# An eight-sequence language-model layer on one core: the first and the last steps reordered, and identity products in TensorE's gaps of the fill

## The reference

```
e0 = E0[tokens]; e1 = E1[tokens]                      # two embedding tables, 75 wide
p0 = e0 @ W0 + b0;  p1 = e1 @ W1 + b1                 # 64 wide
h  = softmax-weighted sum of p0 and p1 (logits p @ Wa + ba)
x  = layernorm(h)
q, k = x @ Q[h], x @ K[h]                             # 8 heads, 32 wide
h += sum over heads of softmax(q k^T / 8) @ x @ VO[h]
x2 = layernorm(h)
H  = gelu(x2 @ W1 + b1)                               # 256 wide
g  = softmax(H @ Wg + bg);  e = argmax(g)             # 8 experts
h += g[e] * (H @ Wd[e] + bd[e])
```

## Time and profile before

| | |
|---|---|
| median of 3 runs | 506.91 us (504.96, 506.91, 508.52) |
| the profiled execution: its own time | 509.85 us |
| its span, first to last instruction | 508.0 us |
| TensorE matmul busy | 461.6 us (91%) |
| VectorE busy | 339.7 us (67%) |
| ScalarE busy | 234.4 us (46%) |
| GpSimd busy | 204.3 us (40%) |
| DMA, mean rate | 61 GB/s |

### The profile page before, as it was taken

How to read it: one execution, slowest core, us unless ns; L and a number is a source line. 1 busy time by engine, 2 the same in 40 slices (tenths; PEclk the granted TensorE clock), 3 DMA queues, 4 the chain that set the end, 5 groups by cost and what they waited for, 6 DMA issues and landing times.

```text
span 508.0 us, 7112 instructions
## 1 busy us (share of the span) xinstructions
PE 461.6 (91%) x1920; PEld 248.5 (49%) x1920; DVE 339.7 (67%) x899; ACT 234.4 (46%) x448; POOL 204.3 (40%) x293
## 2 busy tenths in 40 slices
PE   2258999999899999999999999999999999989674
PEld 2236455455454655455545555555544554435251
DVE  4626857977776777768776778677677766722525
ACT  1012455565634474545644573448354653484020
POOL 8322211531427614462526432762046315521635
PEclk9999999999989999999999999999899999997957
DMA  6053313432232223122322223222212321000000
GB/s 144 0 134 90 76 37 85 115 74 64 64 87 50 65 67 101 34 59 68 84 52 65 63 75 87 65 63 68 69 30 66 81 73 40 10 12 0 1 10 10
DMA packets 24851, 30.94 MB, mean 61 GB/s; under 512 B 9196, under 2 KB 11500, under 8 KB 24812
## 3 DMA queue, kind: packets, MB, share of 16 engines
q1 hardware_dynamic: 22700, 27.25, 21.2%
q0 software_dynamic: 1536, 2.46, 2.1%
q10 hardware_dynamic: 576, 0.79, 0.6%
HBM read 3.99 MB, written 1.05 MB: 10 GB/s over the span
## 4 chain that ended last, share of the span: by engine, by line
PE 81%; DVE 6%; ACT 5%; issue 4%; ACTq 2%; POOL 1%; DMA 1%; SPq 1%; DVEq 0%; POOLq 0%
PE ctx_ps L780 24%; PE s_ps L760 13%; PE st_ps L769 12%; PE sh_ps L850 11%; PE sh_ps L827 6%; PE sh_ps L842 3%; PE sh_ps L804 3%; PE sh_ps L808 3%; PE sh_ps L787 2%; ACT L487 2%; PE sh_ps L809 2%; ACTq L201 1%; PE sh_ps L796 1%; DVE neg_max L512 1%; ACT prob L383 1%
## 5 line engine op out<-in xcount | busy, mean ns | idle before, releaser
L383 ACT ACTIVATE prob<-st_ps 128x512 f32<-128x512 f32 x256 | 138.9, 595 | 139.1 <-PE st_ps L769 137.5
L512 DVE TENSOR_REDUCE neg_max<-s_ps 128x1 f32<-128x512 f32 x256 | 164.7, 683 | 30.6 <-PE s_ps L760 29.4
L780 PE MATMUL ctx_ps<-prob,xa 128*64 128x512 f32 x512 | 140.9, 630 | 0.0
L760 PE MATMUL s_ps<-kst,qst 96*128 96x512 f32 x256 | 113.2, 488 | 6.7 <-DMA kst<-raw_k 4.2
L769 PE MATMUL st_ps<-qst,kst 98*128 98x512 f32 x256 | 86.8, 417 | 3.8 <-ACT prob L383 3.8
L760 PEld LDWEIGHTS s_ps<-kst,qst 96*128 96x128 f32 x256 | 47.9, 202 | 76.0 <-issue 33.1
L308 POOL TENSOR_TENSOR zsum<-z 128x256 f32<-128x256 f32 x31 | 23.0, 742 | 126.7 <-DVE z L595 126.7
L850 PE MATMUL sh_ps<-wd,hid 128*128 128x512 f32 x128 | 63.6, 627 | 0.3 <-DVE z L595 0.3
L769 PEld LDWEIGHTS st_ps<-qst,kst 98*128 98x128 f32 x256 | 50.0, 197 | 26.1 <-ACT prob L383 12.8
L639 DVE TENSOR_TENSOR yb<-sh_ps,bg_bd_s 128x512 f32<-128x512 f32 x32 | 22.1, 690 | 35.9 <-PE sh_ps L850 27.0
L780 PEld LDWEIGHTS ctx_ps<-prob,xa 128*64 128x64 f32 x512 | 25.7, 136 | 40.1 <-issue 32.9
(11 more groups left out here) (90 smaller groups left out, 484.2 us busy)
## 6 DMA issues: line engine op xcount, KB each, us to landing
qst<-raw_q SPq DMA_DIRECT2D x192, 64.0 KB, 2.0
kst<-raw_k SPq DMA_DIRECT2D x180, 64.0 KB, 2.0
qst<-shift_t SPq DMA_DIRECT2D x64, 4.0 KB
out<-res SPq DMA_DIRECT2D x8, 128.0 KB, 1.8
kst<-raw_k ACTq DMA_DIRECT2D x12, 64.0 KB, 2.2
rows<-emb,idx POOLq DMA_INDIRECT x32, 2.9
wd<-WdT SPq DMA_DIRECT2D x1, 512.0 KB, 5.1
w_raw<-weights SPq DMA_DIRECT2D x2, 192.0 KB, 3.8
```

Of the source, the lines that this page charges most:

```text
L383: AC.activation(prob[:, t % P_BUFS, :], st_ps[t % ST_BANKS][:, :], ACT.Exp, scale=-1.0).then_inc(p_done, 1)
L512: V.tensor_reduce(neg_max[:, n:n + 1], s_ps[(NT * b + n) % S_BANKS][:, :], AX.X, ALU.min).then_inc(max_done, 1)
L760: PE.matmul(s_ps[k % S_BANKS][:, :], qst[b % 2][0:3 * R, h, c * P:(c + 1) * P], kst[b % 2][0:3 * R, h, :], start=True, stop=True).then_inc ...
L780: last = PE.matmul(ctx_ps[d * C:(d + 1) * C, :], xa[b % 2][:, c, :], prob[:, (2 * m + d) % P_BUFS, :], start=(c == 0), stop=(c == J - 1))
```

## The change

At the start: the row of -1 in `kst` is written by GpSimd after `xa` of the first sequence and not after the first gather; VectorE builds `vox` (now `head_values`) after its copy of `e1_t` and not before the loop; `q1` and `k1` of sequence 0 are made at step -8 and not at -4, and VectorE takes both their parts; ScalarE's queue issues the keys of head 4 as well; the query stacks of heads 4 and 5 come earlier on SyncE's queue and apart from the key stacks, and sequence 0's `shift` goes ahead of the stacks of its step. The embedding of sequence 1 is done one to two steps later (`e0_t`, `e1_t` at step -2 and not -3; `p0`, `p1` at 0 and not -2), with its `blend` on VectorE and its `normal0` at the head of VectorE's step 2.

At the end: the expert products of sequence 6 are moved to steps 65 and 66, behind the last `vo`, and those of sequence 6 and 7 go into the banks `s_ps` and `st_ps` (`SPARE`), which are free once all maxima and exponentials are done; their evictions are items of their own (`ev0` to `ev3`), for sequence 6 at step 67, behind `normal1` of sequence 7; sequence 7's second layernorm, hidden layer, gate and routing are one step earlier; `yb` has four slots; VectorE takes two of the four mixes of sequence 6 too.

TensorE gets `keep_warm`: fp32 products of the 128x128 identity with itself into `ctx_ps`, which nothing reads before the first context. There are 12 before its loop, 3 after each of the first three quarters of the first `e0_t`, 20 after the first `p1` and 8 after the first `k1`: 49 in all.

```diff
@@ -48,13 +48,25 @@
-OTHERS.update({f"stack{h}": h - 6 for h in range(H)})
+OTHERS.update({f"{name}{h}": h - 6 for name in ("stackq", "stackk") for h in range(H)})
+OTHERS.update({"ev0": 15, "ev1": 16, "ev2": 17, "ev3": 18})
-MOVED = {(name, 1): 3 for name in ("e0_t", "e1_t", "p0", "p1", "logits")}
-MOVED.update({(name, 1): 2 for name in ("alpha", "blend", "moments0", "power0", "normal0", "xa", "x_t", "q0", "k0")})
-MOVED["y1", B - 2] = 1
+MOVED = {("stackq4", 0): -1, ("stackq5", 0): -2, ("q1", 0): -4, ("k1", 0): -4}
+MOVED.update({(name, 1): 5 for name in ("p0", "p1", "logits")})
+MOVED.update({(name, 1): 4 for name in ("e0_t", "e1_t", "alpha", "blend")})
+MOVED.update({(name, 1): 3 for name in ("moments0", "power0", "normal0", "xa")})
+MOVED.update({(name, 1): 2 for name in ("x_t", "q0", "k0")})
+MOVED.update({("y0", B - 2): 2, ("y1", B - 2): 2, ("y2", B - 2): 1})
+MOVED.update({(f"ev{j}", B - 2): 4 - j for j in range(J)})
+MOVED.update({(f"mix{j}", B - 2): 3 for j in range(J)})
+MOVED.update({(name, B - 1): -1 for name in ("moments1", "power1", "normal1", "x2_t", "hid0", "hid1", "gate", "route")})
+
+SPARE = {("y0", B - 2): 0, ("y1", B - 2): 1, ("y2", B - 2): 2, ("y3", B - 2): 3,
+         ("y0", B - 1): 4, ("y1", B - 1): 0, ("y2", B - 1): 1, ("y3", B - 1): 2}
+ON_POOL = {B - 2: (0, 1), B - 1: (0, 2)}
+ON_DVE = ((B - 2, 2), (B - 2, 3), (B - 1, 1), (B - 1, 3))
...
-CLAIMS = [use for s in range(FIRST, LAST) for table in (BEFORE, BEHIND) for use in claims(s, table)]
+CLAIMS = [use for s in range(FIRST, LAST) for table in (BEFORE, BEHIND) for use in claims(s, table) if use not in SPARE]
...
-        yb = sb("yb", [P, 2, NE, C])
+        yb = sb("yb", [P, J, NE, C])
...
+            if (name, b) in SPARE:
+                return (s_ps + st_ps)[SPARE[name, b]]
             return sh_ps[PLACE[name, b] % SH_BANKS]
...
             for s in range(FIRST, LAST):
+                for p in range(PAIRS):
+                    if 0 in due(s, f"shift{p}"):
+                        store_shift(sp, 0, p)
                 for h in range(H):
-                    for b in due(s, f"stack{h}"):
+                    for b in due(s, f"stackq{h}"):
                         stack_queries(sp, b, h)
-                        if b > 0 or h >= HG:
+                    for b in due(s, f"stackk{h}"):
+                        if b > 0 or h > HG:
                             stack_keys(sp, b, h)
                 for p in range(PAIRS):
                     for b in due(s, f"shift{p}"):
-                        store_shift(sp, b, p)
+                        if b > 0:
+                            store_shift(sp, b, p)
...
-            ops = GP if b > 0 else nc.vector
+            ops = GP if b > 1 else nc.vector
...
                     copy_x(pool, b)
+                    if b == 0:
+                        pool.wait_ge(xa_ready, 1)
+                        for n in range(2):
+                            GP.memset(kst[n][3 * R:3 * R + 2, :, :].bitcast(FP32), -1.0).then_inc(minus_ready, 1)
+                            pool.wait_ge(minus_ready, n + 1)
                 for p in range(PAIRS):
                 for b in due(s, "blend"):
-                    if b > 0:
+                    if b > 1:
                         mix_embeddings(pool, b)
                 for b in due(s, "gather"):
                     gather(pool, b)
-                    if b == 0:
-                        for n in range(2):
-                            GP.memset(kst[n][3 * R:3 * R + 2, :, :].bitcast(FP32), -1.0).then_inc(minus_ready, 1)
-                            pool.wait_ge(minus_ready, n + 1)
...
-                            split_high(act, b, g, which)
+                            if b > 0 or g == 0:
+                                split_high(act, b, g, which)
                             if b == 0 and g == 0 and which == "k":
-                                for h in range(HG):
+                                for h in range(HG + 1):
...
+            if b == 0 and g == 1:
+                dve.wait_ge(filled[name], 1)
+                V.tensor_scalar(raw[g][:, 0, :], bank(name, b)[:, :], scale, None, ALU.mult).then_inc(high_ready[name], 1)
             dve.wait_ge(high_ready[name], b + 1)
             V.scalar_tensor_tensor(raw[g][:, 1, :], bank(name, b)[:, :], scale, raw[g][:, 0, :].bitcast(FP32), ALU.mult, ALU.subtract).then_inc(emptied[name], 1)
...
-            if b < B - 1 or j < 2:
-                at_least(dve, res_ready, J * b + j - 1)
-            elif j % 2 == 0:
-                dve.wait_ge(res_ready, J * b + j // 2)
+            if b < B - 1:
+                at_least(dve, res_ready, J * (b - 1) + j + 1)
+            elif j in ON_POOL[b - 1]:
+                dve.wait_ge(res_ready, mixed_before(b - 1, j + 1))
             else:
-                dve.wait_ge(tail_mixed, j // 2)
...
+        def head_values(dve):
+            dve.wait_ge(vox_ready, 1)
+            dve.wait_ge(vo_loaded, VO_ALL)
+            dve.wait_ge(ident_ready, 2)
+            for d in range(2):
+                rows_ = slice(d * C, (d + 1) * C)
+                V.tensor_tensor(vox[rows_, :, d * C:(d + 1) * C], vo_raw[rows_, :, :], vo_base[rows_, :, :], ALU.subtract).then_inc(vox_ready, 1)
+                V.tensor_copy(vox[:, :, 2 * C + d:2 * C + d + 1], ident[:, (d + 1) * C - 1:(d + 1) * C].unsqueeze(1).to_broadcast([P, PAIRS, 1])).then_inc(vox_ready, 1)
 
...
+                if 1 in due(s, "normal0"):
+                    normalise(dve, 1, 0)
+                    low_part(dve, 1, 0)
...
-                for b in due(s, "y1"):
+                        head_values(dve)
                     if b == B - 1:
-                        tail_mix(dve, 1)
+                        tail_mix(dve, b, 1)
...
-                    if b == 0:
+                    if b < 2:
                         mix_embeddings(dve, b)
...
                 for j in (0, 2, 3):
-                    for b in due(s, f"y{j}"):
+                    for b in due(s, f"ev{j}"):
                         y_out(dve, b, j)
-                        if j == 3 and b == B - 1:
-                            tail_mix(dve, j)
+                        if (b, j) in ON_DVE:
+                            tail_mix(dve, b, j)
...
+            if (name, b) in SPARE:
+                pe.wait_ge(max_done, NT * B)
+                pe.wait_ge(p_done, NT * B)
+                if b == B - 1 and name != "y0":
+                    pe.wait_ge(emptied[f"y{int(name[1]) - 1}"], b)
+                return
...
+        def keep_warm(times):
+
+            for _ in range(times):
+                PE.matmul(ctx_ps[:, 0:P], ident[:, :], ident[:, :], start=True, stop=True)
+
...
+                if b == 0 and n == 0 and j < J - 1:
+                    keep_warm(3)
...
             pe.wait_ge(ident_ready, 2)
+            keep_warm(12)
...
                         embed_proj(pe, b, n)
+                        if b == 0 and n == 1:
+                            keep_warm(20)
...
                         project_qk(pe, b, 1, which)
+                        if b == 0 and which == "k":
+                            keep_warm(8)
```

More of the change, by code:

```diff
@@ L230, in store_shift, with mixed_before @@
                              shift_t[p % 2][part * PT:(part + 1) * PT, :].bitcast(FP32)).then_inc(shift_stored[p], 16)
+        def mixed_before(b, j):
+            return sum(k in ON_POOL.get(r, range(J)) for r in range(b + 1) for k in range(J if r < b else j))
         def store_out(sp, b):
-            if b == B - 1:
-                sp.wait_ge(res_ready, J * b + J // 2)
-                sp.wait_ge(tail_mixed, J // 2)
+            if b in ON_POOL:
+                sp.wait_ge(res_ready, mixed_before(b, J))
+                sp.wait_ge(tail_mixed, 2 * (b - B + 3))
             else:
@@ L318, in mix @@
         def mix(pool, b, j):
-            last = b == B - 1
-            if last and j % 2:
+            if j not in ON_POOL.get(b, range(J)):
                 return
@@ L324, in mix @@
             pool.wait_ge(coef_ready, b + 1)
-            before = J * b + (j // 2 if last else j)
+            before = mixed_before(b, j)
             k = 4 * before
@@ L650, in tail_mix @@
+            V.tensor_tensor(yb[:, j, :, :].rearrange("p e c -> p (e c)"), bank(f"y{j}", b)[:, :], bg_bd_s[:, NE:], ALU.add).then_inc(emptied[f"y{j}"], 1)
+        def tail_mix(dve, b, j):
+            y = yb[:, j, :, :]
+            steps = 4 * ON_DVE.index((b, j))
+            dve.wait_ge(emptied[f"y{j}"], b + 1)
+            dve.wait_ge(coef_ready, b + 1)
+            dve.wait_ge(out_stored[b % 2], 16 * (b // 2))
             V.tensor_tensor(y, y, coef[b % 2][:, j, :].unsqueeze(2).to_broadcast([P, NE, C]), ALU.mult).then_inc(tail_step, 1)
@@ L674, in _ @@
             V.tensor_tensor(w_lo[:, :], w_raw[:, :], w_hi[:, :].bitcast(FP32), ALU.subtract).then_inc(w_split, 1)
-            dve.wait_ge(vox_ready, 1)
-            dve.wait_ge(vo_loaded, VO_ALL)
-            dve.wait_ge(ident_ready, 2)
-            for d in range(2):
```

(14 more changed lines are left out.)

22 lines of the change are left out of this document (6 added, 16 removed).

## The result

Over 20 executions the changed kernel takes 502.29 us in the median (496.22 to 505.79), the kernel before 504.94 (503.46 to 508.97). The ratio is 0.989, with a 95% interval of 0.9862 to 0.9919: faster by about 1%, 2.7 us in the medians and 5.5 us by the ratio, where 13.7 was forecast; the median lies outside the forecast range (486 to 500). The ratio compares only the executions within 1.5% of their kernel's fastest, while medians and ranges here are of all executions, so for kernels with a wide spread the two differ by some us and both are given. The median of the kernel before had itself been 2 us too high with three runs.

What follows compares the result with a forecast made beforehand. TensorE's gapless matmul chain bounds the middle, so only the ends' savings count: fill 4.6 + 4.9 - 3.5 - 1 = 5.0 us, end 8.7, sum 13.7, median from 506.91 to 493.2 us, range 486 to 500.

Steps and rivals of the forecast that it cites:

- parts 1 to 3: Fill up to the transposed scores: moved memset, identity products, shorter score stretch; scores 4.6 us earlier, then 4.9 more.
- The memset: Fill: without the memset beside it, the cast of `w_hi` takes about 0.6 us instead of 3.92.
- the unhindered split from PSUM: Fill: VectorE splits `q1` and `k1` beside the moved memset without being held; other bound 3.7 us.
- the path of the shift: Fill, scores to transposed scores: maxima, transposes, row, copy, issues and landing of the first shift, about 12.5 us.
- part 4: Sequence 1's `p0`, `p1` move into full step 0, cost 3.5 us; VectorE's chain to `x_t` costs 1 more, bounds 0 and 5.
- part 3: Fill, from scores to first transposed scores: 17.4 us shrinks to about 12.5, gain 4.9 us.
- Rival 2: The clock rises in the fill and stays up through the scores: 486 us; chance 0.15.
- Rival 4: Slower: the clock falls more often in the middle, at each of seven gates for 6.8 us: 510 us; chance 0.04.
- parts 5 to 7: End: `y0` moved, second layernorm unhindered, gate and expert products sooner; gain 8.7 us, bounds 7 and 11.

Runs made afterwards that it cites:

- e5: The kernel of e2 without its 49 identity products; 498.37 us.
- e2: The changed kernel with the embedding of sequence 1 back at the early steps of the kernel before; 495.85 us, ratio 0.9815.
- e1: The changed kernel without its 49 identity products; 505.73 us, ratio 0.9912.
- e6: The changed kernel with only the projections p0 and p1 of sequence 1 moved from step 0 to step -1; 494.59 us, ratio 0.9747.
- e11: The kernel of e4 with sequence 1's embedding late as in the change, its blend on VectorE, normal0 at the head of step 2; 506.51 us, ratio 1.0008.
- e4: The fill of the kernel before with the change's new end, spare banks and four slots of yb; 497.73 us, ratio 0.9838.
- e12: The kernel of e6 with 8 identity products (16 records of 128 columns) in step 0, in place of the 16 narrow ones; 502.36 us, ratio 0.9889.
- e10: The changed kernel with six identity products in the step of each gate; 501.04 us, ratio 0.9927.
- e3: The changed kernel's fill, with the end's order as in the kernel before and yb at four slots; 510.44 us, ratio 0.991.
- e8: The kernel of e2 with one identity product behind each score matmul of steps -4 to -1, 15 in all; 499.98 us, ratio 0.9889.
- e7: The kernel of e2 with six identity products in the step of each gate; 494.21 us, ratio 0.9768.
- e9: The kernel of e6 with the six identity products per gate of e7; 497.96 us, ratio 0.9883.

## Why the prediction was wrong

**The fill up to step 0, parts 1 to 3: right, with two sizes off.** Forecast 9.5 us, measured 9.8. The memset (0.56 us for 3.92), the unhindered split from PSUM (0.69), the path of the shift (11.0 us from scores to transposed scores, forecast 12.5) came as worked out. The start of the scores was forecast 4.6 us earlier and came 3.5, because the last gather was there at 11.55 and not at 10.28, which put the end of the projections at 14.8 and not at 13.2. The identity products were put at about 5 us; with them and without, the medians differ by 2.5 (e5 and e2) and 3.4 us (e1 and the change), the ratios by 1.9 and 1.1.

**Two steps failed.** Set against the forecast, the profiled execution gained 9.8 us up to the transposed scores (forecast 9.5), lost 7.3 from there to the first context copy (forecast 4.5), lost 5.3 in the middle (forecast 0) and gained 9.3 at the end (forecast 8.7).

**The first is part 4**, "Cost 3.5. [...] Bounds 0 and 5; I take 1", against 3.5 us that part 3 counted as saved by taking `p0` and `p1` out of the stretch before. So the move was to cost 1 us on balance. Pairs of kernels show that it saves much less and costs more; the first four differ in the move, the last in other work in the same place (times in us; "scores to copy" is from the first transposed scores to the first context copy of the profile; "by ratios" is the difference of the ratios times 505 us):

| with / without that work | transposed scores | scores to copy | medians | by ratios |
|---|---|---|---|---|
| the change / e2 | 41.66 / 42.73 | 24.0 / 18.8 | +6.4 | +3.8 |
| the change / e6 | 41.66 / 42.79 | 24.0 / 19.2 | +7.7 | +7.2 |
| e1 / e5 | 43.08 / 44.05 | 25.3 / 20.6 | +7.4 | +3.0 |
| e11 / e4 | 48.16 / 50.40 | 25.0 / 17.0 | +8.8 | +8.6 |
| e12 / e6 | 40.91 / 42.79 | 19.9 / 19.2 | +7.8 | +7.2 |

In the fill the projections lie in waits, so that taking them out saves 1.0 to 1.1 us (2.2 in the old fill) and not 3.5. Behind the transposed scores the move costs 4.7 to 8.0 us (the first four pairs), and whole times are longer by 3.0 to 8.8 in all five. The work itself was sized right (3.52 us in the profile). What I left out is that it stands where TensorE has just entered the full stretch at the lower level: the time at that level after the first transposed scores is 17.0 us in the change and 8.4 before, and in e11 the low stretch ends at 71.5 us and not at 59.5. I had priced only the work, and kept the end of the slow stretch where it was. Where an execution has the clock up in step 0 all the same, the first copy is not late (61.06 in e10, 60.82 in e12), but TensorE then waits for VectorE's chain in step 2 (3.53 and 3.38 us): the chain takes what the clock gives. e12 also shows that it isn't a matter of narrow products.

**The second is the premise** that a change at the two ends moves the time by what it takes off there, which put the middle at nothing. From the first context copy to the last, less half the time at the lower level, the profiles of the eleven kernels without products at the gates take 394.2 to 396.8 us. So the middle's work is the same, and what changes is how long the clock is down in it: 20.5 us of that stretch in the change, 6.8 in e4 and e6. Against the kernel before, this cost the change 5.3 us up to the copies of sequence 7, more than part 4 was off by.

**Rival 2 was mispriced.** It was to bring 7 us more. e10's profile is near that case, and its first copy is 4.6 us earlier than the changed kernel's, by the wait for VectorE's chain.

**Rival 4**, the slower one, was the right mechanism with too small a chance (0.04). I argued that nothing in the middle changes; the program didn't, but the executions did (17.1 us at the lower level between 65 and 450 us, before 6.8). e4 has no such loss with the same middle, so it isn't from the slots of `yb` and seems to come with the work in step 0 (e11, e12 and the change: 13.7, 17.0 and 17.1 us; e2, e5 and e6: 6.8, 0 and 0). But e3, late too, had 10.3, e1 only 3.4, and e8, early, 10.3, so with one profile each this is a tendency, and that the work sets off these falls is not shown. Filling the gates' gaps leaves 3.4 us in each of three profiles (e7, e9, e10), and raises the mean clock of all executions in each of three pairs (0.959 to 0.965, 0.959 to 0.963, 0.946 to 0.955), but the products cost 0.64 us a gate: the medians moved by -1.6 (e7 and e2), -1.3 (e10 and the change) and +3.4 us (e9 and e6).

**The end, parts 5 to 7: right.** Forecast 8.7 us, 8.1 by e4 alone. The transposes follow the head sum by 5.0 us; the products of sequence 6 run under VectorE's layernorm; the clock fell at the gate at 483.8 and was back at 490.6, shorter than before, as expected.

**The parts in whole times.** The end alone brings 8.1 us in the medians (e4), the early fill 1.9 more (e2 against e4, 497.7 and 495.9), and the late embedding takes 6.4 away. These three add up to the change's gain because they are differences of the same medians, so that is no test of them. The early fill keeps only a third of its 5.9 us at the first copy (67.39 to 61.52); in the two profiles most of the rest goes into two falls that e4's execution didn't have. The forecast's 5.0 us for the fill as changed came as nothing reliable (e3).

What stays open is why executions of the kernels with that work in step 0 spread over 8 to 17 us and those of e2, e4, e7, e8 and e9 over 4 to 6 (e5 and e6 lie between, 10 to 11; the former have 10 to 20 executions each, the latter 6), and whether and how work in step 0 sets off falls 80 us later. Much of the spread goes with the clock: in e12 the span runs from 492.3 us at a mean clock of 0.970 to 509.6 at 0.926, in e6 from 488.6 at 0.970 to 498.9 at 0.945.

## What to carry to other kernels

When a step is moved into a stretch that runs at the lower clock, price it by what it does to the time of the rise, not by its own length; here 3.5 us of work, counted as 1 us on balance, cost 3 to 9. Work that fits into waits of the fill is best left there, even if it delays the first full step by 1 us: e2 and e6 beat both kernels, 495.9 and 494.6 us, by undoing one of the change's parts. A middle that nothing in the program touches is no constant either: take its time at the lower level from several executions before an end is credited with its whole gain. Products that fill a gap are work too; where TensorE is full, count them. And read the level of the clock from the spacing of equal matmuls, since the page shows nothing before its first mark.

## What the runs showed of the hardware

A cast between SBUF tiles on VectorE beside a memset on GpSimd took 3.92 us (the kernel before), without it 0.56 (the change). A tensor_scalar from PSUM beside that memset took 0.69 us, as long as the copy of `e1_t` from PSUM without one. The subtraction that gives `w_lo`, with both its inputs in SBUF, took 0.96 us beside the memset and without.

At the gate of sequence 6 the clock fell for 6.8 us in e2, behind a gap of 1.33 us on TensorE, 2.0 us of full-width products and 2.1 us of 8-column products. With 1.6 us of full-width products in the gap it didn't fall in e7, and fell for 3.4 us in e9 and e10. In the change's fill it fell at 23.0 us, after 4.7 us of gapless full-width products, a gap of 2.85 us and the four transposes of `x_t`. A fall of 3.4 us with TensorE full cost 1.6 us: the gates of sequences 2 and 3 follow each other in 55.95 us with one between them (the change) and in 54.4 without (e6).
